# The rotation loop's products as 64x64 tiles, three to a level, and the chunk's products at other places in the level

## What is computed

```python
def step(mat, t):
    i, j, theta = t
    c = jnp.cos(theta); s = jnp.sin(theta)
    ri = mat[i]; rj = mat[j]
    mat = mat.at[i].set(c * ri - s * rj)
    mat = mat.at[j].set(s * ri + c * rj)
    return (mat, None)
...
mat, _ = jax.lax.scan(step, mat0, (idx_i, idx_j, rots))
return x @ mat.T
```

## Time and profile before

| | |
|---|---|
| median of 3 runs | 7918.79 us (7906.65 to 7920.52) |
| the profiled execution | 7903.8 us, span 7902.0 us |
| busy in the span | PE 61%, DVE 68%, POOL 56%, ACT 16% |
| the rotation loop | about 852 to 2311 us of the span |

### The profile page before, as it was taken

The page is one execution under the profiler, slowest core; times in us unless marked ns, Lnnn a source line. Parts: engine busy times, 40 slices in busy tenths (PEclk is TensorE's granted clock), DMA queues, the critical chain, the costliest instruction groups (busy, mean ns, idle before and its releaser), DMA issues. The chain is left out here.

```text
span 7902.0 us, 174461 instructions
## 1 busy us (share of the span) xinstructions
PE 4781.0 (61%) x58063; PEld 3939.6 (50%) x58063; DVE 5336.5 (68%) x12256; ACT 1288.0 (16%) x2955; POOL 4441.6 (56%) x3974
## 2 busy tenths in 40 slices
PE   0000577777855355468888678888688787355551
PEld 0000576767743244347777567776477775233331
DVE  7999655555548455657777467775577774578878
ACT  0000111121210111112222112221122221122210
POOL 5888777771000577317777257774277770177730
PEclk9999878888875555589999899999899998655555
DMA  0000000000010444246664166661467640244420
GB/s 27 1 4 1 1 1 1 1 1 0 0 28 5 111 131 132 77 122 193 197 193 118 43 190 197 195 185 32 132 193 199 193 108 12 50 114 111 110 74 16
DMA packets 708566, 691.55 MB, mean 88 GB/s; under 512 B 234981, under 2 KB 589355, under 8 KB 708165
## 3 DMA queue, kind: packets, MB, share of 16 engines
q0 software_dynamic: 227328, 446.06, 20.8%
q1 hardware_dynamic: 480846, 240.51, 11.0%
HBM read 766.03 MB, written 77.58 MB: 107 GB/s over the span
## 5 line engine op out<-in xcount | busy, mean ns | idle before, releaser
L1601 POOL DMA_INDIRECT kvring<-kvtab,oth x1776 | 1984.3, 1117 | 825.4 <-issue 425.6
L1001 POOL DMA_INDIRECT e_hg<-htab,oth_d x992 | 1015.4, 1024 | 1478.0 <-issue 1420.8
L1652 PE MATMUL ea_pss<-ea_qb,ea_kT 128*128 128x128 f32 x7104 | 1018.9, 276 | 0.0
L1652 PEld LDWEIGHTS ea_pss<-ea_qb,ea_kT 128*128 128x128 f32 x7104 | 945.1, 194 | 16.1
L1722 DVE TENSOR_TENSOR acc<-ea_psg,acc 128x64 f32 x1776 | 399.3, 225 | 611.9 <-PE ea_psg L1663 538.6
L1696 ACT ACTIVATE ea_kT<-ea_pst 128x512 f32<-128x512 f32 x888 | 482.1, 595 | 2023.0 <-PE ea_pst L1640 2006.8
L1640 PE MATMUL ea_pst<-ident,kvring 128*128 128x128 f32 x3552 | 489.2, 281 | 474.7 <-DMA kvring<-kvtab,oth 473.7
L1640 PEld LDWEIGHTS ea_pst<-ident,kvring 128*128 128x128 f32 x3552 | 385.8, 142 | 553.1 <-DMA kvring<-kvtab,oth 343.4
L240 POOL DMA_INDIRECT steps<-or_rec,or_rplacei x392 | 566.9, 1446 | 135.5 <-issue 135.5
L1736 DVE TENSOR_REDUCE ea_sc<-ea_pss 128x64 f32<-128x1024 f32 x444 | 540.7, 1218 | 48.1 <-PE ea_pss L1652 48.1
L1764 DVE TENSOR_TENSOR ea_mix<-ea_hot,ea_att 128x1024 f32<-128x1024 f32 (+1 forms) x444 | 544.9, 1227 | 0.1
(11 more groups left out here) (508 smaller groups left out, 9761.1 us busy)
## 6 DMA issues: line engine op xcount, KB each, us to landing
ea_qb<-qtab SPq DMA_DIRECT2D x1776, 64.0 KB
qtab<-at_qst SPq DMA_DIRECT2D x75, 512.0 KB, 3.3
kvring<-kvtab,oth POOLq DMA_INDIRECT x1776
e_stack<-ohtab SPq DMA_DIRECT2D x744, 32.0 KB
kvtab<-at_kvst SPq DMA_DIRECT2D x75, 256.0 KB, 2.7
e_hg<-htab,oth_d POOLq DMA_INDIRECT x992
ea_mk<-mtab SPq DMA_DIRECT2D x444, 3.0 KB
htab<-Hd SPq DMA_DIRECT2D x2, 3200.0 KB, 13.4
```

Source lines behind the costliest of these rows:

```text
L1001: pool.indirect_dma_start(out=hg[:, b % RING, u, :], out_offset=None, in_=htab, in_offset=bass.IndirectOffsetOnAxis(ap=oth[:, b * 4 + u:b ...
L1601: pool.indirect_dma_start(out=kv[:, b % R, u, :], out_offset=None, in_=kvtab, in_offset=bass.IndirectOffsetOnAxis(ap=oth[:, b * QB + u:b * ...
L1652: mm = pe.matmul(ps_s[r % 2][:, u, k * 2 * HN:(k + 1) * 2 * HN], kT[:, r % 2, u, k, :], qb[:, r, u, :], start=False, stop=True, skip_group ...
```

## The change

The products of the levels work on 64x64 blocks: of each chunk, the early half with itself and the late half with itself, side by side on opposite quarters of the PE array. Names with `[at, ...]` are those halves, on partitions 0 to 63 or 64 to 127. A level is now three products of such blocks: X' = A T (`level`, `ps_v`, copied by ACT into `X`), then T' X and X T' into the two parts of `ps_w` (`closed`). A single mask for the left part and no `Lm` remain, `Am` is a quarter as large a level, and `la`, `T` and `S` have two buffers (their places in the diff are left out). `T`'s first level for the next batch is computed inside the batch before it. The two joins go to `ps_R` with tiles of 64x64, and TF is written straight from the last sums.

The chunk's products move: `ahead` (R M) stands behind `closed`, `applied` (S Y) behind the next level's first product. On PE each group of small tiles has an increment of a semaphore `turns` in front, for which nothing waits. The columns of numbers are masked with HS in place of CS, with HL = 5 rounds in place of six.

```diff
--- before.py
+++ after.py
...
-        link(dve.tensor_tensor(la[:, :, :], la[:, :, :], lb[:, :, :], ALU.add))
+    def joined(link, h):
+        link(dve.tensor_tensor(la[:, h], la[:, h], lb[:, :, :], ALU.add))
         dve.sem_inc(s["l"], 1)
-    def levels(link, h):
-        for c in range(CB):
-            ins = dve.tensor_tensor(Lm[:, h, c], la[:, c, :].unsqueeze(1).broadcast_to([P, LV, P]), mask[:, :, :], ALU.mult)
+        for at in (early, late):
+            ins = dve.tensor_tensor(T[at, h, :, 0, :], la[at, h, :, at],
+                                    mask[at, :].unsqueeze(1).broadcast_to([CS, CB, CS]), ALU.mult)
         link(ins)
     def turned(link, b, h):
         dve.wait_ge(s["turn"], b + 1)
-        for c in range(CB):
-            ins = dve.tensor_tensor(Am[:, h, c], ps_a[:, c, :].unsqueeze(1).broadcast_to([P, LV, P]), maskT[:, :, :], ALU.mult)
+        link(dve.tensor_tensor(T[:, h, :, 1, :], ps_a[:, :, :],
+                               maskT[:, 0, :].unsqueeze(1).broadcast_to([P, CB, CS]), ALU.mult))
+        link(dve.tensor_tensor(T[:, h].rearrange("p c k n -> p (c k) n"), T[:, h].rearrange("p c k n -> p (c k) n"),
+                               B["eye"][:, :].unsqueeze(1).broadcast_to([P, 2 * CB, CS]), ALU.add))
+        for v in range(1, HL):
+            ins = dve.tensor_tensor(Am[:, v - 1], ps_a[:, :, :],
+                                    maskT[:, v, :].unsqueeze(1).broadcast_to([P, CB, CS]), ALU.mult)
         link(ins)
+        dve.sem_inc(s["ti"], 1)
+    def added(b, h, v):
+        dve.wait_ge(s["w"], b * HL + v)
+        dve.tensor_tensor(T[:, h], ps_w[:, :, :, :], T[:, h], ALU.add).then_inc(s["tt"], 1)
...
             link = loop_linker(dve, s["chain3"], b, NCH)
+            parameters(link, b + 1, g)
+            dve.wait_ge(s["tt"], b * 3 + 1)
+            added(b, h, 2)
+            copied(b, 0)
+            dve.tensor_tensor(S[:, h], K["row"][:, :].unsqueeze(1).broadcast_to([P, CB, D]),
+                              own[:, h, :].unsqueeze(2).broadcast_to([P, CB, D]), ALU.is_equal).then_inc(s["S"], 1)
             dve.wait_ge(s["r"], b + 1)
-            for kind, left in ((0, Lm), (1, Am)):
-                for at in (early, late):
-                    ins = dve.tensor_tensor(T[at, :, kind, :], left[at, h, :, 0, at],
-                                            B["eye"][at, :].unsqueeze(1).broadcast_to([CS, CB, CS]), ALU.add)
-                    if kind == 0 or at == early:
-                        link(ins)
-            ins.then_inc(s["tt"], 1)
-            for v in range(1, HL):
-                copied(b, v - 1)
-                if v == 1:
-                    parameters(link, b + 1, 1 - h)
-                if v == 2:
-                    rights(link, 1 - h)
-                if v == 3:
-                    lefts(link, b + 1, 1 - h)
-                if v == 4:
-                    levels(link, 1 - h)
-                dve.wait_ge(s["w"], b * HL + v)
-                dve.wait_ge(s["tt"], b * HL + v)
-                dve.tensor_tensor(T[:, :, :, :], ps_w[:, :, :, :], T[:, :, :, :], ALU.add).then_inc(s["tt"], 1)
-            dve.wait_ge(s["tt"], b * HL + HL)
-            link(dve.tensor_copy(TF[early, :, early], T[early, :, 1, :]))
-            link(dve.tensor_copy(TF[late, :, late], T[late, :, 1, :]))
-            dve.sem_inc(s["tz"], 1)
-            turned(link, b + 1, 1 - h)
-            dve.wait_ge(s["m"], b * CB + CB)
-            dve.tensor_tensor(S[:, :, :], K["row"][:, :].unsqueeze(1).broadcast_to([P, CB, D]),
-                              own[:, h, :].unsqueeze(2).broadcast_to([P, CB, D]), ALU.is_equal).then_inc(s["S"], 1)
+            dve.wait_ge(s["row"], b + 2)
+            lefts(link, g, (0, 1))
+            lefts(link, g, (2, 3))
+            dve.wait_ge(s["tt"], b * 3 + 2)
+            added(b, h, 3)
+            copied(b, 1)
+            joined(link, g)
+            rights(link, g, (0, 1), False)
+            dve.wait_ge(s["tt"], b * 3 + 3)
+            dve.wait_ge(s["w"], b * HL + 4)
+            dve.tensor_tensor(TF[late, :, late], ps_w[late, :, 1, :], T[late, h, :, 1, :], ALU.add).then_inc(s["tl"], 1)
+            dve.tensor_tensor(T[early, h, :, 0, :], ps_w[early, :, 0, :], T[early, h, :, 0, :], ALU.add).then_inc(s["te"], 1)
+            dve.tensor_tensor(TF[early, :, early], ps_w[early, :, 1, :], T[early, h, :, 1, :], ALU.add).then_inc(s["tz"], 1)
+            copied(b, 2)
+            turned(link, b + 1, g)
+            copied(b, 3)
+            rights(link, g, (2, 3), False)
+            added(b + 1, g, 1)
+            rights(link, g, (), True)
...
-    def turn(b):
+    def turn(b, h):
         pe.wait_ge(s["l"], b + 1)
+        pe.sem_inc(s["turns"], 1)
         for c in range(CB):
-            tr = pe.transpose(ps_a[:, c, :], la[:, c, :], K["ident"][:, :])
-        tr.then_inc(s["turn"], 1)
+            for at in (early, late):
+                mm = pe.matmul(ps_a[at, c, :], la[at, h, c, at], K["ident"][at, at], start=True, stop=True,
+                               skip_group_check=True)
+        mm.then_inc(s["turn"], 1)
+    def level(h, v):
+        pe.sem_inc(s["turns"], 1)
+        for c in range(CB):
+            for at in (early, late):
+                mm = pe.matmul(ps_v[at, c, :], Am[at, v - 1, c, :], T[at, h, c, 0, :], start=True, stop=True,
+                               skip_group_check=True)
+        mm.then_inc(s["v"], 1)
+    def closed(h):
+        pe.sem_inc(s["turns"], 1)
+        for c in range(CB):
+            for at in (early, late):
+                pe.matmul(ps_w[at, c, 0, :], T[at, h, c, 1, :], X[at, c, :], start=True, stop=True, skip_group_check=True)
+        for c in range(CB):
+            for at in (early, late):
+                mm = pe.matmul(ps_w[at, c, 1, :], X[at, c, :], T[at, h, c, 1, :], start=True, stop=True,
+                               skip_group_check=True)
+        mm.then_inc(s["w"], 1)
...
             b = i * 2 + h
-            for v in range(1, HL):
-                pe.wait_ge(s["tt"], b * HL + v)
-                for c in range(CB):
-                    for kind, left in ((0, Am), (1, Lm)):
-                        mm = pe.matmul(ps_v[:, c, kind, :], left[:, h, c, v, :], T[:, c, kind, :], start=True, stop=True,
-                                       skip_group_check=True)
-                mm.then_inc(s["v"], 1)
-                ahead(b, v - 1)
+            g = 1 - h
+            for v in range(2, HL):
+                pe.wait_ge(s["tt"], b * 3 + v - 1)
+                level(h, v)
                 if v == 2:
-                    rows(b + 1, 1 - h)
+                    rows(b + 1, g)
+                else:
+                    applied(b, g, v - 3)
+                pe.wait_ge(s["vs"], b * HL + v)
+                closed(h)
                 if v == 4:
-                    turn(b + 1)
-                pe.wait_ge(s["vs"], b * HL + v)
-                for c in range(CB):
-                    for kind in range(2):
-                        mm = pe.matmul(ps_w[:, c, kind, :], V[:, c, 1 - kind, :], T[:, c, kind, :], start=True, stop=True,
-                                       skip_group_check=True)
-                mm.then_inc(s["w"], 1)
-                applied(b, v - 1)
-            pe.wait_ge(s["tt"], b * HL + HL)
+                    turn(b + 1, g)
+                ahead(b, v - 2)
+            pe.wait_ge(s["tl"], b + 1)
+            pe.sem_inc(s["turns"], 1)
             for c in range(CB):
-                mm = pe.matmul(ps_v[:, c, 1, :], Lm[:, h, c, HL, :], T[:, c, 1, :], start=True, stop=True,
-                               skip_group_check=True)
+                mm = pe.matmul(ps_R[0][early, c // 2, c % 2, 0:CS], la[late, h, c, early], TF[late, c, late],
+                               start=True, stop=True, skip_group_check=True)
             mm.then_inc(s["v"], 1)
+            applied(b, g, CB - 2)
+            ahead(b, CB - 1)
+            pe.wait_ge(s["ti"], b + 2)
+            level(g, 1)
+            pe.wait_ge(s["te"], b + 1)
             pe.wait_ge(s["vs"], b * HL + HL)
+            pe.sem_inc(s["turns"], 1)
             for c in range(CB):
-                mm = pe.matmul(ps_w[0:CS, c, 1, :], T[:, c, 0, :], VX[:, c, :], start=True, stop=True,
-                               skip_group_check=True)
+                mm = pe.matmul(ps_R[1][early, c // 2, c % 2, 0:CS], T[early, h, c, 0, :], VX[early, c, :],
+                               start=True, stop=True, skip_group_check=True)
             mm.then_inc(s["w"], 1)
-            pe.wait_ge(s["rs"], b + 1)
             pe.wait_ge(s["tz"], b + 1)
+            pe.wait_ge(s["vs"], b * HL + HL + 1)
+            closed(g)
+            applied(b, g, CB - 1)
             pe.wait_ge(s["tx"], b + 1)
...
+    def product(b, v):
+        act.wait_ge(s["v"], b * HL + v)
+        act.activation(X[:, :, :], ps_v[:, :, :], ACT.Copy).then_inc(s["vs"], 1)
     def kept(k, c):
         act.wait_ge(s["m"], k * CB + c + 1)
@@ -713,19 +754,21 @@
```

(18 more changed lines are left out.)

85 lines of the change are left out of this document (45 added, 40 removed).

## The result

The changed kernel takes 7445.53 us (median of 4 runs, 7434.61 to 7446.86), the kernel before 7917.26 (7906.65 to 7920.52): a ratio of 0.9403, 95% interval 0.9387 to 0.942, so 472 us less. The profiled execution takes 7434.6, its span 7432.8.

A forecast was written before the change was run, and what follows sets the result against it. The prediction took the rotation loop to end the first phase; at 27 us a batch it ends at 1729, leaving GpSimd's scatters as the end, 501.6 us saved: 7903.8 becomes 7402, median 7417, range 7380 to 7620.

The forecast's parts named there:

- the case named: First phase: GpSimd's scatters end it instead of the rotation loop; total 7385 to 7440 us, chance 0.66.
- GpSimd becomes the end: First phase: the loop ends near 1729 us, before GpSimd's scatters at 1808.6, saving 501.6 us; chance 0.66.
- The price of a tile: PE in the loop: 224 64x64 instructions a batch at 0.029 us each, 6.5 us.
- no overlap: Rival, PE's small tiles: 0.06 us each, mixed clock, 38.3 us a batch, 7699 us; range 36 to 45 a batch, 0.11.
- a full price: Rival, PE's small tiles: each costs 0.112 us like a full one, 54.4 us a batch, 8214 us; slower has 0.05.
- Switches: PE in the loop: tile sizes alternate 16 times a batch, up to 0.24 us each, 3.8 us a batch.
- The period: Time of one batch of the rotation loop: 45.0 us before, 26.4 by calculation, taken as 27.
- the walk: Loop calculation: instruction prices in each engine's order, steps starting when semaphores allow; 26.4 us a batch at 2.4 GHz.
- The clock stays at the upper level: PE in the loop: longest wait 1.4 us, so 2.4 GHz is kept; 1.2 GHz would give 39.3 us a batch.
- Every P up to 29.5 gives one time: First phase: any batch time P up to 29.5 us leaves GpSimd as the end, so the total is the same.
- Lm, a long DVE instruction, goes, but other DVE work gets denser. I take the rate as it is: GpSimd's sort scatters in the first phase: their rate stays 1.338 us each; the undisturbed floor is 62 us earlier.
- The rest of the sum: After the last scatter's start at 1805.5 us: next phase at 1809.5, profiled execution 7402, median 15.0 above it.

The follow-up runs named there:

- one_sort: The changed kernel without the 392 scatters of the second sort: 7216.2 us; the next phase issues at 1667.7 instead of 1834.7 us, later phases not comparable.
- unpaired: The changed kernel with the small products of all early halves first, then the late halves, instead of alternating pairs: 7438.0 us, 26.8 us a batch.
- closed_twice: The changed kernel with every group of closing products written twice, 128 more 64x64 instructions a batch: 7395.8 us, 27.9 us a batch.
- before_new_places: The kernel before, full-size products kept, with only the chunk's products (R M, S Y) at the change's places: 7666.1 us, ratio 0.9685, 37.3 us a batch.
- long_wait: The changed kernel with three DVE memsets ahead of T's level 3 sum, making PE wait once a batch: 7440.6 us, 30.7 us a batch.

## Why the prediction was right, and where not

The forecast was 7417 with a range of 7380 to 7620, the likeliest case 7385 to 7440; it came to 7445.5. Inside the range, the case named, 5 us above its own range.

- *GpSimd becomes the end* (0.66): shown, by the end of the phase and by *one_sort*.
- *The price of a tile*, 0.029 in pairs from `ea_psg`: shown by the trace, and that it comes of the overlap by *unpaired*. Both rivals, no overlap and a full price, are out. The bound for no overlap, 0.06, is what a quarter alone does take (0.058).
- *Switches*, up to 0.24 us each: ahead of small groups PE's loads sat idle for "issue" 98.4 us in 96 groups and 68.9 in 96, 0.7 to 1.0 each, but mostly under waits for other engines. Where PE waits for nothing, the last small instruction of a group starts 0.15 us ahead of the first full one (1304.52, then L668 at 1304.67), where small ones of one quarter follow each other after 0.058; the other way it is 0.21 (1303.38, then L656 at 1303.59) against 0.112. So a switch costs some 0.1 us, an estimate from these starts, under half of the bound. No run had fewer switches.
- *The period*, 26.4 by the walk and 27 as taken: 25.1. For *closed_twice* the walk let 2.8 of the added 3.7 us through, and 2.8 came. It took DVE as the long engine with 22.0 us of work, the gaps between its instructions included; DVE was busy 75% of 25.1, so 18.9, without them. For *unpaired* 28 to 29.5 were expected and 26.8 came, as the halves still overlap where they meet; for *before_new_places* 41 were expected and 37.3 came.
- *The clock stays at the upper level*: 1.00, and *long_wait* shows a wait that brings it down.
- *"Every P up to 29.5 gives one time"*: false. *closed_twice* has a longer period and ends its phase 29 us earlier.
- *"Lm, a long DVE instruction, goes, but other DVE work gets denser. I take the rate as it is"*: the step with the wrong size. The rate went from 1.338 to 1.366, 22.0 us over 784 scatters. Lm's 19.0 us of lengthening did go, but the join and S went from 6.6 us to 43.1. They take no longer than before, but all 32 batches now lie beside the scatters instead of 21, and the batch's beat and the scatters' fall into step: a scatter started 0.31 us into the join in batch after batch, and all 32 joins hit one, for 0.79 us on average.
- The rest of the sum: from the last scatter's start to the next phase 7.1 us where 4.0 were taken (as much in the other kernels whose phase GpSimd ends; what fills it was not looked into); the later phases took 7.3 us more than in the profile of before (5598.1 against 5590.9, from the next phase's first issue to the end of the span). The change does not touch them, and in the other runs the same stretch took 5588.6 to 5607.7 (*one_sort* apart), so 7.3 is inside what it varies by. 7402 + 22.0 + 3.1 + 7.3 = 7434.4, measured 7434.6. The median lies 10.9 above the profiled execution, not 15.0.
- *The prediction's account of the gain* named the tiles and the lists and gave the places no term. That holds for the new lists (-0.8 us), and not for the old ones, where the places alone bring 250 us.
